# Preactivated residual block of three convolutions: the first convolution two images in front, and the last two images interleaved

## The reference, cut to what matters

```python
# x: (8, 32, 128, 128) float32; L0: 3x3 weights; L1: two filters of the same small support
def _L0_conv_ref(x, weight, bias):            # int8-valued convolution
    qx, sx = _quantize_per_tensor(x)          # sx = max|x| over ALL images; q = round(x*127/sx)
    qw, sw = _quantize_per_tensor(weight)
    out = conv(qx, qw) * (sx * sw / (127*127))
    return out + bias
def _instnorm_lrelu(x):                       # mean and variance over one image and channel
    xn = (x - mu) * rsqrt(var + 1e-5);  return where(xn >= 0, xn, 0.2 * xn)
def _L1_conv_ref(image, weight1, weight2):
    h = _instnorm_lrelu(_disco_conv(image, weight1))
    return _instnorm_lrelu(_disco_conv(h, weight2))
x = x + _L0_conv_ref(_gn(x), L0_conv_weight, L0_conv_bias)   # _gn: group norm, 16 groups per image
x = x + _L1_conv_ref(_gn(x), L1_conv_weight1, L1_conv_weight2)
```

## Time and profile before

| | |
|---|---|
| median of the three timed runs | 407.02 us |
| the profiled execution itself | 405.03 us |
| its span, first to last instruction | 403.1 us |
| granted TensorE clock, mean | 0.976 of full speed |
| PE busy | 310.0 us (77%) |
| DVE busy | 280.1 us (69%) |
| ACT busy | 229.7 us (57%) |
| POOL busy | 162.7 us (40%) |

### The profile page before, as it was taken

The page is one execution under the profiler, slowest core; times in us unless marked ns, Lnnn a source line. Parts: engine busy times, 40 slices in busy tenths (PEclk is TensorE's granted clock), DMA queues, the critical chain, the costliest instruction groups (busy, mean ns, idle before and its releaser), DMA issues.

```text
span 403.1 us, 11804 instructions
## 1 busy us (share of the span) xinstructions
PE 310.0 (77%) x5344; PEld 128.7 (32%) x5344; DVE 280.1 (69%) x418; ACT 229.7 (57%) x239; POOL 162.7 (40%) x240
## 2 busy tenths in 40 slices
PE   0000100567999999999999999999999999997970
PEld 0000100426343334334333433333343334333520
DVE  3739899792287499569857965995697499557144
ACT  1079996354252775484576628645853775385434
POOL 0189867105833807351661537074334800100000
PEclk9999999996999999999999999999999999998995
DMA  7999400000000022005001300400050022005005
GB/s 270 398 425 424 195 1 1 2 0 2 2 3 2 3 119 94 2 2 211 2 3 68 146 2 2 182 31 2 3 210 3 2 107 106 2 3 210 2 2 208
DMA packets 4177, 34.78 MB, mean 86 GB/s; under 512 B 608, under 2 KB 768, under 8 KB 1280
## 3 DMA queue, kind: packets, MB, share of 16 engines
q1 hardware_dynamic: 4128, 34.04, 20.7%
HBM read 17.26 MB, written 16.78 MB: 84 GB/s over the span
## 4 chain that ended last, share of the span: by engine, by line
PE 60%; DVE 28%; POOL 4%; DMA 3%; issue 2%; ACT 1%; SPq 0%; DVEq 0%; POOLq 0%
PE ring L820 44%; PE ring L872 8%; DVE amax L631 8%; DVE xs L713 7%; DVE bn_c L696 7%; PE ring L826 3%; DMA xs<-w_dram 3%; PE ring L779 2%; POOL apad L486 2%; PE gathered_in L772 1%; DVE bn_x L686 1%; DVE xs L680 1%; DVE bn_x L609 1%; ACT scaled L333 1%; POOL xs L425 1%
## 5 line engine op out<-in xcount | busy, mean ns | idle before, releaser
L696 DVE BATCH_NORM_STATS2 bn_c<-ring 128x6 f32<-128x512 f32 x128 | 82.8, 688 | 79.5 <-PE ring L826 79.5
L339 ACT COPY apad<-ring 128x1024 f32<-128x1024 f32 x32 | 32.2, 1006 | 62.8 <-DVE bn_c L696 62.8
L820 PE MATMUL ring<-hpad,own 64*32 64x512 f32 x512 | 67.0, 592 | 0.0
L826 PE MATMUL ring<-apad,own 64*32 64x512 f32 x512 | 66.9, 591 | 0.0
L826 PE MATMUL ring<-hpad,own 64*32 64x512 f32 x512 | 66.9, 592 | 0.0
L820 PE MATMUL ring<-apad,own 64*32 64x512 f32 x512 | 66.8, 590 | 0.0
L826 PE MATMUL ring<-apad,side 64*32 64x512 f32 x512 | 66.6, 587 | 0.0
L820 PE MATMUL ring<-hpad,vert 64*32 64x512 f32 x512 | 66.4, 587 | 0.0
L820 PE MATMUL ring<-apad,vert 64*32 64x512 f32 x512 | 66.4, 587 | 0.0
L826 PE MATMUL ring<-hpad,side 64*32 64x512 f32 x512 | 66.4, 587 | 0.0
L454 POOL TENSOR_SCALAR var_eps_c<-moments_c 128x1 f32<-128x1 f32 x16 | 3.0, 190 | 121.1 <-DVE moments_c L604 120.6
(11 more groups left out here) (111 smaller groups left out, 500.7 us busy)
## 6 DMA issues: line engine op xcount, KB each, us to landing
xs<-x_dram SPq DMA_DIRECT2D x8, 2048.0 KB, 9.8
out_dram<-xs SPq DMA_DIRECT2D x14, 1024.0 KB, 3.9
out_dram<-xs SPq DMA_DIRECT2D x4, 512.0 KB, 2.8
xs<-w_dram SPq DMA_DIRECT2D x1, 288.0 KB, 10.2
const<-const_dram SPq DMA_DIRECT2D x1, 146.0 KB, 2.5
xs<-w_dram SPq DMA_DIRECT2D x1, 36.0 KB, 1.8
bias<-bias_dram SPq DMA_DIRECT2D x1, 0.5 KB, 2.3
```

What stands on the lines that cost most here:

```text
L339: nc.scalar.copy(unit_of(tile, u), grid(slot(FIRST[v] + u))).then_inc(taken[v], 1)
L696: ins = nc.vector.bn_stats(bn[s][:, u * UBANKS + h, :], ring[:, (FIRST[v] + u) % SLOTS, h, :])
L820: nc.tensor.matmul(bank_out(u, v, hp, C * (2 * px + py), C), wv[q0:q0 + 64, v - 1, px, py, :], window(tile, u * UBANKS + hp, dy, 0, q0, 64 ...
L826: ins = nc.tensor.matmul(bank_out(u, v, hx, C * (2 * px + py), C), ws[q0:q0 + 64, v - 1, px, py, :], window(tile, u * UBANKS + hx, 0, dx, ...
```

## The change

Convolution 0 of images 0 and 1 both run before the periods, and the periods 0 to 5 hold convolution 1 of t, convolution 0 of t + 2 and convolution 2 of t. The end is written out by itself: convolution 1 of image 6, convolution 1 of 7, convolution 2 of 6, convolution 2 of 7. Image 7 gets tiles of its own for this: `h_last` lies in `xs` over images 0 and 1, `a_last` over images 2 and 3, once POOL has seen their stores end (`stored_first`) and has zeroed the borders. Image 1 is scaled by ACT into `hpad` (`affine_one`) and rounded by POOL in two operations per piece (`round_one`) into `q_one`, a 16-bit view of `apad[1]`. Scale and shift get two columns, by turns of the image. The slot of a unit and the wait for it are worked out from one list, `ORDER`. Both uses of `keep_clock` between convolutions are dropped; the one ahead of the first convolution stays.

```diff
+        q_one = apad[1][:].rearrange("p r c -> p (r c)").bitcast(F16)[:, 0:PAD * PAD].rearrange("p (r c) -> p r c", c=PAD)
+        h_last = xs[:, 0:PAD * PAD].rearrange("p (r c) -> p r c", c=PAD)
+        a_last = xs[:, 2 * COLS:2 * COLS + PAD * PAD].rearrange("p (r c) -> p r c", c=PAD)
...
-        FIRST = {1: 0, 0: UNITS, 2: 2 * UNITS}
+        ORDER = [(0, 0), (0, 1)]
+        for t in range(B - 2):
+            ORDER += [(1, t), (0, t + 2), (2, t)]
+        ORDER += [(1, B - 2), (1, B - 1), (2, B - 2), (2, B - 1)]
...
+            def affine_one(n):
+                r0, r1 = EDGES[n:n + 2]
+                nc.scalar.activation(flat(hpad)[:, r0 * BLK:r1 * BLK], xs_rows(1, r0, r1), ACT.Identity,
+                                     bias=q_shift[:, 1:2], scale=q_scale[:, 1:2]).then_inc(q_one_scaled, 1)
...
+            def round_one(n):
+                r0, r1 = EDGES[n:n + 2]
+                rows = flat(hpad)[:, r0 * BLK:r1 * BLK]
+                pool.wait_ge(q_one_scaled, n + 1)
+                nc.gpsimd.tensor_scalar(rows, rows, 1.0, ROUND, ALU.mult, ALU.add).then_inc(q_one_step, 1)
+                pool.wait_ge(q_one_step, n + 1)
+                nc.gpsimd.tensor_scalar(rows_of(q_one, r0, r1), grid(rows), 1.0, -ROUND, ALU.mult, ALU.add
+                                        ).then_inc(q_one_ready, 1)
...
+                if t == B - 4:
+                    pool.wait_ge(stored_first, 16 * 8)
+                    zero_border(a_last).then_inc(last_zero, 1)
+                    zero_border(h_last).then_inc(last_zero, 1)
...
+            def wait_slot(v, b, u):
+                n = place(v, b, u) - SLOTS
+                if n >= 0:
+                    v0, b0 = ORDER[n // UNITS]
+                    pe.wait_ge(taken[v0], UNITS * b0 + n % UNITS + 1)
...
-                elif now:
-                    gather("c1", t)
-                    pe.wait_ge(taken[1], UNITS * t + 2)
-                    keep_clock(KEEP_H, 1)
...
+            for u in range(UNITS):
+                conv0_pair(0, u)
+            conv0_pair(1, 0)
+            conv0_pair(1, 1)
+            conv0_pair(1, 2)
+            gather("x1", 0)
+            conv0_pair(1, 3)
             pe.wait_ge(weights12_ready, 1)
-            for t in range(B + 1):
-                period(t)
+            for t in range(B - 2):
+                conv(1, t, gather_early=("c2", t - 1) if t >= 1 else None)
+                conv0_pair(t + 2, 0, gather_after=("x1", 1) if t == 0 else None)
+                conv0_pair(t + 2, 1, gather_after=("c1", t))
+                conv0_pair(t + 2, 2)
+                conv0_pair(t + 2, 3)
+                conv(2, t, gather_late=("x1", t + 2))
+            conv(1, B - 2, gather_early=("c2", B - 3))
+            conv(1, B - 1, gather_early=("c1", B - 2))
+            conv(2, B - 2, gather_early=("c1", B - 1))
+            conv(2, B - 1, gather_early=("c2", B - 2))
+            gather("c2", B - 1)
```

More of the change, by code:

```diff
@@ L367, in norm_out @@
                 act.wait_ge(taken[2], UNITS * t + u + 1)
-                rows = unit_of(apad[t % 2], u)
-                nc.scalar.activation(rows, rows, ACT.Prelu, bias=shift["c2"][:], scale=scale["c2"][:],
+                rows = unit_of(a_tile(t), u)
+                nc.scalar.activation(rows, rows, ACT.Prelu, bias=param(shift["c2"], t), scale=param(scale["c2"], t),
                                      alpha=SLOPE).then_inc(out_norm, 1)
             def period(t):
-                before, now, after = t >= 1, 0 <= t < B, t + 1 < B
+                before = t >= 1
                 if before:
@@ L381, in period @@
                     norm_out(t - 1, 2)
[L382 to L383 removed]
+                take(1, t, 1, hpad)
                 if before:
                     norm_out(t - 1, 3)
[L386 to L395 removed]
@@ L396, in period @@
-                if now:
-                    take(2, t, 2, apad[t % 2])
-                if after:
-                    make_a(t + 1, 2)
-                    make_a(t + 1, 3)
+                take(1, t, 2, hpad)
+                take(1, t, 3, hpad)
+                for n in range(4):
+                    make_h(t, n)
+                take(2, t, 0, apad[t % 2])
+                take(2, t, 1, apad[t % 2])
+                make_a(t + 1, 0)
+                make_a(t + 1, 1)
+                take(2, t, 2, apad[t % 2])
@@ L404, in _ @@
                 affine0(n)
+            for n in range(4):
+                affine_one(n)
             act.wait_ge(kern_done, 1)
@@ L407, in _ @@
             assemble(kern[:, 1], own12[:, 1], side12[:, 1], vert12[:, 1], None).then_inc(weights12_ready, 1)
-            for t in range(-1, B + 1):
+            for n in range(4):
+                make_a(0, n)
+            for t in range(B - 2):
                 period(t)
+            last_periods()
         @block.gpsimd
@@ L762, in _ @@
             for n in range(4):
                 rounded(0, n)
-            for t in range(-1, B + 1):
+            x1_unit(0, 0)
+            x1_unit(0, 1)
+            x1_stats(0, 0)
+            x1_unit(0, 2)
+            x1_unit(0, 3)
+            x1_stats(0, 1)
+            x1_stats(0, 2)
+            x1_stats(0, 3)
+            spread_stats("x1", 0)
+            group_moments("x1", 0)
+            for u in range(UNITS):
+                x1_unit(1, u)
+            for u in range(3):
+                x1_stats(1, u)
@@ L765, in _ @@
+            conv_stats(1, 0, 0)
+            x1_stats(1, 3)
+            spread_stats("x1", 1)
+            for t in range(B - 2):
                 period(t)
+            last_periods()
         @block.tensor
```

335 lines of the change are left out of this document (200 added, 135 removed).

## The result

| | before | after |
|---|---|---|
| median of the timed runs | 406.28 us (405.12 to 407.77, 4 runs) | 390.19 us (389.68 to 391.34, 4 runs) |
| profiled execution | 405.03 us | 390.26 us |
| its span, mean granted clock | 403.1 us, 0.976 | 388.4 us, 0.984 |

The ratio is 0.962, with a 95% interval of [0.9595, 0.9644]: the change takes 15.4 us off (14.5 to 16.5); the two medians lie 16.1 apart. The forecast was 391.0.

The account below looks back on a forecast made before the run. PE's matmuls were taken as the bound from period 1 on. New start, periods and end gave a 387.05 us span, 16.05 less than 403.1; 405.03 less that is 389.0, plus 1.99 makes 391.0, range 388.6 to 394.7.

Parts of the forecast that it names:

- Head: Up to convolution 1 of image 0: image 1's convolution 0 fills the first gap, start at 97.2 instead of 98.81.
- Period 0: First period: 35.76 us as before plus 0.47 for one more small matmul, for x1 of image 1.
- periods 1 to 5: Steady periods: order on every engine unchanged, 36.42 us each, 182.1 in all; convolution 1 of image 6 starts at 315.5.
- The end: From convolution 1 of image 6: three convolutions of 14.26 without waits, last count 15.4 into the fourth, then 13.35 us.
- rival B: Last four convolutions: ACT holds the ring, costing up to 5 us, for 392 to 396; chance 0.07.
- The DVE term of 1.3: Last convolution: image 6's outputs between DVE's counts delay the last count, 15.4 us after its start against 14.08; 1.3 us lost.
- Rival A: Head pause: the clock falls and about 4 us run at half rate, 2.0 us more, 393.0; chance 0.22.
- no fall in the forecast: Head pause, 92.0 to 95.4: the forecast of 391.0 has the clock stay full despite only one small matmul.
- The row at the end of before: Clock evidence from the old kernel's end: it fell at 394.4, over 4 us after the last convolution; pointed to 391.0.
- the 1.99 us: Final sum: the median lay 1.99 us above the profiled execution, taking the forecast from 389.0 to 391.0.
- 8.3 us to the last gap: Before the last convolution 2: PE's gap of waiting and idle matmuls vanishes, a gain of about 8.3 us.
- one convolution 0 less in the periods: Periods: one convolution 0 moves out of them into the head, a gain of 7.8 us.

Follow-up runs that it names:

- e4_pool_alone: Changed kernel with POOL alone quantising image 1, three operations per piece, without ACT's four pieces; 393.94 us, ratio 0.9704 to the kernel before.
- e8_no_reduce: e4_pool_alone without the maximum over partitions; DVE copies each partition's own maximum, so values are not the reference's; 388.43 us, ratio 0.9568 to the kernel before.
- after_again: The changed kernel run once more with no edit; 390.28 us, ratio 0.9613 to the kernel before.
- e3_out_late: Changed kernel with outputs 2 and 3 of image 6 moved behind DVE's last moments; 391.26 us, ratio 0.9634 to the kernel before.
- e6_keep_and_gate: e2_keep_head with output 3 of image 6 held until POOL has made the last scale and shift; 389.76 us, ratio 0.96 to the kernel before.
- e9_split_store: e6_keep_and_gate with image 6 stored in four parts instead of two; 388.04 us, ratio 0.9561 to the kernel before.
- e2_keep_head: Changed kernel plus 24 idle matmuls before and 24 behind image 0's small matmul in the head pause; 389.06 us, ratio 0.9584 to the kernel before.
- e1_one_by_one: Changed kernel's head and periods, but images 6 and 7 one after the other at the end; 405.6 us, ratio 0.9988 to the kernel before.
- e5_shared_a: Changed kernel with image 7's a back in the shared apad[1] instead of its own tile; 395.64 us, ratio 0.9737 to the kernel before.

## Why the prediction was right

**Head.** Units 0 to 2 from 86.08, the small matmul at 92.99, unit 3 at 94.88: each within 0.7 us of the forecast. Unit 3 came 0.5 earlier than 95.4: the small matmul started 0.2 earlier than in the profile of before, and it took 0.40 us at the full clock, where the forecast had kept the 0.62 of the half clock. POOL's pieces came when they were said to, partly by luck: its start was set by the delay shown by `e4_pool_alone` and `e8_no_reduce`, not by ACT's piece, and this was not in the working. Nor was PE alone the bound of unit 2, as forecast: it started at 89.79, behind POOL's third piece (88.59 + 1.05), and in `after_again` PE waited 0.20 us for that piece. Convolution 1 of image 0 started at 97.69 instead of 97.2.

**Period 0 and periods 1 to 5.** From 97.69 to 134.55 is 36.86, against 36.23 forecast; the 0.63 above it is the rest of the half-rate stretch. The periods were 36.43 for 36.42. Convolution 1 of image 6 was forecast for 315.5 and started at 316.78: 1.6 for the clock and 0.1 for the periods, less 0.5 for the earlier unit 3.

**The end.** Three convolutions took 42.76 us for 42.8; no wait for ACT, so rival B did not occur. The last count came 15.40 behind its convolution for 15.4, the end 13.46 behind that for 13.35. The DVE term of 1.3 was sized right. `e3_out_late` and `e6_keep_and_gate` won 0.8 of it at the last count and lost it again, the one to the delay on GpSimd and the other to the stores; `e9_split_store` kept most of it.

**Clock.** Rival A, at 0.22, is what happened, in both profiles of this kernel. Its size was 2.0; it measured 1.6 in the trace (0.93 in unit 3 and 0.67 in period 0, against `e2_keep_head`) and 1.2 between the medians. The step of the prediction that failed is the choice of no fall in the forecast. The row at the end of before showed a fall over 4 us after the last convolution; it gave no reason to think that a pause of 3.4 us is safe. The prediction did not use a nearer row of the same trace. It is the last gap of the kernel before, PE by microsecond (stretch, length, busy, clock, DMA), and its small matmul:

```profile
367.00:368.00 1.00, 0.56 (x16) 1.00 0.97 393
...
370.00:371.00 1.00, 0.56 (x4) 0.66 0.97 401
```

```profile
370.44 0.60 PE L772 MATMUL gathered_in<-spread_c,const 128*128 128x12 f32 x2 [2.88 <-DVE spread_c L705]
```

PE stopped at about 367.6, and the clock had fallen at about 370.3, before the small matmul (both estimates from the shares in these rows). That is 2.8 us without a matmul, less than the pause that the forecast took as safe. The rule of the Trainium skill that rival A names held: unit 3 and the start of convolution 1 ran at half clock, for 1.6 us.

**The sum.** 387.05, less 0.5 for unit 3, plus 1.6 for the clock, 0.1 for the periods and 0.1 for the end, gives the 388.4 of the span. The median nevertheless came out 0.8 under the forecast. The forecast had added the 1.99 us by which the median of three runs lay above the profiled execution (with the fourth run, 405.12, it is 1.25); in the kernel after, the profiled execution (390.26) lies at the median (390.19). An error of 1.3 us one way and one of 2.1 the other cancelled in part, which is luck; between profiled executions the gain was 14.8 us for 16.05 forecast.

**Attribution.** The forecast gave 8.3 us to the last gap, 7.8 to one convolution 0 less in the periods and 1.6 to the head. `e1_one_by_one` shows how to read that: the terms are not separate gains. Without the alternation they add up to 0.1% (interval -0.1 to 0.4%). With it the rest of the time comes off. The alternation without the early convolution 0 was not run, since it needs image 7's x1 ahead of convolution 2 of image 6.

## What to carry to other kernels

Independent work that fills a wait is a fixed stock: moving it to another gap opens one where it was. Here the gaps vanished only when two chains, the last two images, each waited behind the other's work. That needed tiles of its own for image 7: the one for a was worth about 4.5 us, the one for h was not tested. Ahead of the end, look at what else runs in the last microseconds: an addition on DVE can delay a one-element operation on GpSimd, and a delayed store can outlast the arithmetic it waited for.

## What the runs showed of the hardware

- GpSimd's first tensor operation behind a maximum over the partitions came 6.9 us after its last border (76.3 to 83.2), with the operands there; without the reduction it followed after 0.1 us. The fills of borders in between were not held up (the last one at 76.00 in `e4_pool_alone`).
- The granted clock fell from 2.4 to 1.2 GHz around a pause of 3.15 us in which PE did one small matmul (91.73 to 94.88), about 0.7 us after PE had begun to work again, and came back at about 99.1. In `after_again` it fell 0.3 us after. In `e5_shared_a` a wait of 2.54 us with no matmul in it was followed by the fall 0.8 us after work had resumed. In `e8_no_reduce` a pause of 2.5 us with one small matmul in it was not followed by a fall. Two blocks of 24 idle matmuls held the clock.
- Two 128x1024 additions of DVE with both inputs in SBUF made two one-element GpSimd operations 0.9 us longer each (0.19 to 1.11, 0.55 to 1.47).
- While DVE rounded image 0 to 16 bits, two of GpSimd's twelve operations on image 1 took longer in `e8_no_reduce`: 1.58 instead of 1.10 and 1.62 instead of 1.20 us.
- The stores at the end ran at 406 to 410 GB/s with a DMA share of 1.01; one megabyte held back to that moment put the end 4.6 instead of 3.4 us behind the last output (`e6_keep_and_gate`), half a megabyte did not (`e9_split_store`). In `e3_out_late` the same megabyte did not either: it went out at 379.3, and image 7's first output ended only at 382.7.
